# A fused decoder layer on one core: another order of instructions in the prologue, in odd self-attention turns, at the transition, in the cross maxima, at the seam and at the end

## The reference

```python
x = x + self_attention(layernorm(x), Wq, bq, Wk, bk, Wv, bv, Wo)      # 16 heads of 16; scores[0,-1] = scores[-1,0] = -1e9
q, k, v = heads(layernorm(x) @ Wq + bq), heads(ctx @ Wk + bk), heads(ctx @ Wv + bv)
energy = where(mask == 0, -1e10, q k^T / 4)
x = x + merge(softmax(energy, axis=1) @ v) @ Wo + bo                   # axis 1: over the heads
gate, up = nvfp4_linear(layernorm(x), gate_w), nvfp4_linear(layernorm(x), up_w)     # 256 -> 1024
x = x + nvfp4_linear(silu(gate) * up, down_w)                          # 1024 -> 256
```

## Time and profile before

| what | value |
|---|---|
| median of 3 runs | 567.04 us (565.94 to 567.5) |
| profiled execution, its own time | 565.97 us |
| its span | 564.2 us |
| instructions | 14,568 |
| PE, DVE, ACT, POOL busy (share of the span) | 93%, 89%, 59%, 60% |

### The profile page before, as it was taken

One profiled execution on the slowest core, in us unless ns is written; L12 is line 12 of the kernel. 1 busy time (PEld: TensorE's weight loads), 2 busy tenths in 40 slices (PEclk: granted clock), 3 DMA queues, 4 the chain that ended last, 5 costly groups with the idle time before them and its releaser, 6 DMA issues. The chain is left out here.

```text
span 564.2 us, 14568 instructions
## 1 busy us (share of the span) xinstructions
PE 523.3 (93%) x6022; PEld 374.5 (66%) x6031; DVE 499.7 (89%) x678; ACT 335.6 (59%) x559; POOL 336.4 (60%) x258
## 2 busy tenths in 40 slices
PE   7899999999899999999999999999999877878876
PEld 7777767777567777777776777777777543444433
DVE  5788888899889888889899999899889999989997
ACT  3755655655555665468475765676568464856644
POOL 3121324323327776767888879977898894745660
PEclk9999999999999999999999999999999998989998
DMA  8910000000110011101110111011100000000001
GB/s 216 319 68 2 3 1 3 3 2 1 42 40 1 12 40 48 46 4 50 49 30 21 49 48 34 18 48 48 35 17 9 9 2 17 0 21 19 20 19 57
DMA packets 16644, 20.77 MB, mean 37 GB/s; under 512 B 2821, under 2 KB 14322, under 8 KB 16578
## 3 DMA queue, kind: packets, MB, share of 16 engines
q1 hardware_dynamic: 14800, 19.18, 11.4%
q10 hardware_dynamic: 1778, 0.66, 0.6%
HBM read 16.16 MB, written 1.84 MB: 32 GB/s over the span
## 5 line engine op out<-in xcount | busy, mean ns | idle before, releaser
L435 POOL TENSOR_TENSOR work<-work,rden 125x1792 f32<-125x1792 f32 x48 | 172.5, 3593 | 3.8
L1045 ACT ACTIVATE work<-scores 125x896 f32<-125x896 f32 x96 | 88.9, 987 | 89.1 <-PE scores L1548 89.1
L715 DVE TENSOR_REDUCE negmax<-scores 125x112 bf16<-125x1792 f32 x48 | 97.1, 2023 | 17.9 <-PE scores L1538 17.2
L723 DVE TENSOR_REDUCE den<-work 125x56 f32<-125x896 f32 x96 | 102.5, 1067 | 7.7 <-ACT work L1045 7.5
L433 POOL TENSOR_TENSOR rden<-rden,stays 125x112 f32<-125x112 f32 x48 | 21.9, 457 | 62.9 <-DVE rden L728 62.8
L1538 PE MATMUL scores<-qz,kT 32*125 32x224 f32 x768 | 49.8, 373 | 3.6 <-ACT work L1045 2.9
L1574 PE MATMUL head_out<-work,v 125*32 125x112 f32 x1536 | 48.7, 265 | 0.3 <-POOL work L435 0.3
L1645 PE MATMUL wide<-ctxT,ck 128*128 128x375 f32 x128 | 48.6, 500 | 0.0
L1548 PE MATMUL scores<-negmax,identb 125*125 125x448 bf16 x192 | 45.4, 359 | 2.5 <-DVE negmax L715 2.2
L1659 PE MATMUL wide<-cv,ctxT 128*125 128x256 f32 x192 | 46.7, 379 | 0.0
L728 DVE RECIPROCAL rden<-den 125x112 f32<-125x112 f32 x48 | 40.9, 852 | 1.4
(11 more groups left out here) (283 smaller groups left out, 1132.3 us busy)
## 6 DMA issues: line engine op xcount, KB each, us to landing
ctx_sb<-in_ctx SPq DMA_DIRECT2D x16, 375.0 KB
mask_sb<-in_mask_Bx1xSxS_if SPq DMA_DIRECT2D x16, 164.1 KB, 5.5
xsx<-in_x SPq DMA_DIRECT2D x4, 448.0 KB, 10.0
out_x<-ores SPq DMA_DIRECT2D x6, 256.0 KB, 2.4
a_raw_w<-in_L_ffn_gate_w SPq DMA_DIRECT2D x1, 1024.0 KB, 8.7
a_raw_w<-in_L_ffn_up_w SPq DMA_DIRECT2D x1, 1024.0 KB, 11.2
a_raw_w<-in_L_ffn_down_w SPq DMA_DIRECT2D x1, 1024.0 KB, 13.3
xt<-xsx SPq DMA_DIRECT2D x4, 112.0 KB, 2.2
```

Of the source, the lines that this page charges most:

```text
L435: pool.tensor_tensor(ex2[0:KP, kc], ex2[0:KP, kc], over, ALU.mult).then_inc(s["prob"], 1)
L715: dve.tensor_reduce(negmax[0:KP, :], scores[0:KP, :, 0:4 * TOK].rearrange("p j (h t) -> p t j h", h=4), AX.XY, ALU.max, negate=True).then_ ...
L723: link(dve.tensor_reduce(den[0:KP, kc, half], ex2[0:KP, kc, :, half, :].rearrange("p g t s -> p t g s"), AX.XY, ALU.add))
L1045: act.activation(ex2[0:KP, kc, 4 * i:4 * i + 4].rearrange("p (j m) t s -> p j m s t", m=NE), scores[0:KP, 2 * i:2 * i + 2, 0:4 * TOK].rear ...
```

## The change

Nothing is computed in another way. Six places get another order.

- **Prologue.** The statistics, rstd and shift of batch 0 are made alone, ahead of the other three of its group (`first_statistics`, `first_shift`, semaphores `stats0`, `rstd0`, `shift0`: four more DVE instructions and one more on POOL). ACT normalises batch 0 before it copies any weight, and copies the weights of keys and values after `a_input_copy(0)`; PE waits for the first weight alone before the queries. The 16 idle products between the weight transposes and the first `a_input_T` are gone. `bias_products` and the copy of `bv_row` come one batch earlier. The values of batch 1 are copied by DVE, between `statistics(2)` and `statistics(3)`, and no longer by ACT.
- **Odd self turns** (5 to 15). The value product is cut in its two halves: the first stands before `maxima_T`, the second where both stood.
- **Transition.** ACT's `maxima_copy(15)` stands before `keys(0, 0)`, and PE's `key(0, 1, ·)` before `a_project(14)`.
- **Cross maxima.** DVE's `key_max(now, 0)` always stands before `head_sum(old, 2, 0)`. Before, it stood behind it in the turns in which no weight or tile work had been put in, which are n = 1, 2, 3, 4, 6 and 13.
- **Seam.** In turn 0 PE's `score(0, 1)` stands before `a_project(15)`, and `less_max(0, 1)` before the query and the first key of batch 1. In turn 15 DVE's `residual(14)` stands behind `inverse(15, 2)`, and both halves of `project(14)` before `less_max(15, 2)`.
- **End.** `output(4)` stands behind `rounded_last`, the end of the DVE's last rounding, and not in k = 7. The down product of pair 5 goes into a bank of its own (`y_before`), so that it doesn't wait for `output(4)`.

```diff
+def of_group(g):
+    return range(max(g * XG, 1), (g + 1) * XG)
 ...
+pool.wait_ge(a_s["stats0"], 1)
+pool.tensor_tensor(rstd[:, 0:1, 0], varp[:, 0:1], minus_half[:, 0:1], ALU.pow).then_inc(a_s["rstd0"], 1)
 for g in range(4):
     pool.wait_ge(a_s["stats"], g + 1)
-    part = slice(g * XG, (g + 1) * XG)
+    part = slice(of_group(g)[0], (g + 1) * XG)
 ...
+first_statistics()
 statistics(0)
+first_shift()
 shift(0)
 ...
 if t == 1:
     statistics(2)
+    dve.wait_ge(a_s["v_ps"], 2)
+    dve.tensor_copy(a_v[:, 1, :, 0:3:2, :], two_heads(value_ps(1))).then_inc(a_s["v"], 1)
     statistics(3)
 ...
-if old and not late:
-    head_sum(old, 2, 0)
 if now:
     key_max(now, 0)
-if old and late:
+if old:
     head_sum(old, 2, 0)
 ...
 inverse(final, 2)
+residual(in_turn(B - 2))
 hidden(0, 1)
 ...
-if k >= 3:
+if 3 <= k < NPT:
     output(k - 3)
 ...
 rounded_last()
+output(NPT - 3)
 output(NPT - 2)
 output_last(0)
 output_last(1)
 ...
+a_normal(0)
 weight_copy(0, wqT)
-weight_copy(1, wkT)
-a_normal(0)
-weight_copy(2, wvT)
 a_input_copy(0)
+weight_copy(1, wkT)
+weight_copy(2, wvT)
 ...
+maxima_copy(b)
+if t == B + 1:
     keys(in_turn(0), 0)
-maxima_copy(b)
 ...
-idle_products(16, ho_ps[:, 0:P], identb[:])
 ...
-if a == 0 and p < NPT - 1:
+if a == 0 and p < NPT - 2:
     wait(pe, s["out"], p)
+y = y_last[a] if p == NPT - 1 else (y_before if p == NPT - 2 else y_ps)[:, a, :]
 ...
 a_input_T(1)
+bias_products()
 first_projections(1)
+pe.wait_ge(a_s["bv_row"], 1)
 maxima_T(0)
 a_value(1)
 score_columns(0)
 a_input_T(2)
-pe.wait_ge(a_s["mT"], 1)
-bias_products()
 ...
+if other:
+    a_value(t, [0])
 maxima_T(b)
 ...
 if other:
-    a_value(t)
+    a_value(t, [1])
+if t == B + 1:
+    key(in_turn(0), 1, 0)
+    key(in_turn(0), 1, 1)
 a_project(b - 1)
-if t == B + 1:
-    key(in_turn(0), 1, 0)
-    key(in_turn(0), 1, 1)
 ...
+if n in (0, B - 1):
+    score(now, 1)
 if n == 0:
     a_project(B - 1)
-if n == B - 1:
-    score(now, 1)
 ...
 if new:
     input_T(new)
     context_T(new)
+if n == 0:
+    less_max(now, 1)
 if new:
     query(new)
     key(new, 0, 0)
-if now:
+if n > 0 and now:
     less_max(now, 1)
```

More of the change, by code:

```diff
@@ L180, in decoder_layer @@
         a_s = {n: sem("a_" + n) for n in (
-            "made", "aux", "rows", "link_d", "link_p", "stats", "rstd", "shift", "w_ps", "w_sb", "bv_cols", "bv_ps",
+            "made", "aux", "rows", "link_d", "link_p", "stats0", "rstd0", "shift0", "stats", "rstd", "shift", "w_ps", "w_sb", "bv_cols", "bv_ps",
             "bv_row", "xn", "biased", "xnT_ps", "xnT", "qk_ps", "pair_q_ps", "pair_q", "pair_k_ps", "qz", "v_ps", "v", "s1_ps", "max", "mT_ps", "mT", "s2_ps",
@@ L251, in decoder_layer @@
         y_ps = small[:].rearrange("p (a d) -> p a d", a=2)
+        y_before = scores[:, 0].rearrange("p (a d) -> p a d", a=2)
         y_last = (scores[:, 2, 0:D], head_out[:, 0:D])
@@ L901, in output @@
                     wait(dve, stored[p % 2], 16 * (p // 2))
-                    dve.scalar_tensor_tensor(out=ores[:, p % 2], in0=y_ps, scalar=alpha[:, 2:3],
+                    dve.scalar_tensor_tensor(out=ores[:, p % 2], in0=y_before if p == NPT - 2 else y_ps, scalar=alpha[:, 2:3],
                                              in1=xt[:, 2 * p:2 * p + 2, :], op0=ALU.mult, op1=ALU.add
@@ L1031, in a_normal @@
                 def a_normal(b):
-                    act.wait_ge(a_s["shift"], b // XG + 1)
+                    if b == 0:
+                        act.wait_ge(a_s["shift0"], 1)
+                    else:
+                        act.wait_ge(a_s["shift"], b // XG + 1)
                     wait(act, a_s["xnT_ps"], b - 1)
@@ L1252, in _ @@
                 a_normal(2)
+                act.wait_ge(a_s["bv_ps"], 1)
+                act.copy(bv_row[:], a_y_ps).then_inc(a_s["bv_row"], 1)
                 maxima_copy(0)
                 a_queries_keys(1)
-                a_values(1)
                 a_input_copy(2)
@@ L1259, in _ @@
                 a_values(2)
-                act.wait_ge(a_s["bv_ps"], 1)
-                act.copy(bv_row[:], a_y_ps).then_inc(a_s["bv_row"], 1)
                 a_normal(3)
@@ L1507, in a_project, with a_value @@
                     last.then_inc(a_s["y_ps"], 1)
-                def a_value(b):
-                    if b >= SINGLE and b % 2 == 1:
+                def a_value(b, part=range(NE)):
+                    if b >= SINGLE and b % 2 == 1 and 0 in part:
                         pe.wait_ge(a_s["v"], b)
-                    for c in range(NE):
+                    for c in part:
                         last = pe.matmul(value_ps(b), a_xnT[:, c, b % 2, :], wvT[:, c, :], start=(c == 0), stop=(c == NE - 1))
-                    last.then_inc(a_s["v_ps"], 1)
+                    if NE - 1 in part:
+                        last.then_inc(a_s["v_ps"], 1)
                 acts, projects, wide_uses, pieces_read = Count(), Count(), Count(), Count()
@@ L1773, in down @@
                             small_free()
+                    y = y_last[a] if p == NPT - 1 else (y_before if p == NPT - 2 else y_ps)[:, a, :]
                     for c in range(FF // P):
-                        last = pe.matmul(y_last[a] if p == NPT - 1 else y_ps[:, a, :], hT[:, a, c, :], downT[:, c, :],
+                        last = pe.matmul(y, hT[:, a, c, :], downT[:, c, :],
                                          start=(c == 0), stop=(c == FF // P - 1))
@@ L1781, in first_projections @@
                     if t == 0:
+                        pe.wait_ge(a_s["w_sb"], 1)
+                    projected(t, 0, wqT)
+                    if t == 0:
                         pe.wait_ge(a_s["w_sb"], 2)
-                    projected(t, 0, wqT)
                     projected(t, 1, wkT)
@@ L1888, in _ @@
                         context_T(new)
+                    if n == 0:
+                        less_max(now, 1)
+                    if new:
                         query(new)
@@ L1914, in _ @@
                         project(old, 0)
+                    if n == B - 1:
+                        project(old, 1)
                     if now:
@@ L1926, in _ @@
                     if old:
-                        for c in range(0 if n < 6 else 1, NE):
+                        for c in range(0 if n < 6 else NE if n == B - 1 else 1, NE):
                             project(old, c)
```

28 lines of the change are left out of this document (16 added, 12 removed).

## The result

The changed kernel takes 569.46 us (median of 11 runs, 568.15 to 572.3), the one before 565.98 (11 runs, 565.47 to 567.5). The ratio is 1.0055, 95% interval 1.0042 to 1.0069: slower, by more than a measurement leaves open. The two profiled executions have spans of 567.6 and 564.2, so the profile holds the whole difference (+3.4).

The account below looks back on a forecast made before the run. TensorE was taken to bound cross attention and the self turns, VectorE the feed forward and the prologue's second part. The terms -0.1, 0, -1.5, +1.1, +0.4, -0.3, +0.7 gave +0.3 on 567.04, so 567.3 us, range 565.0 to 569.7.

Parts of the forecast that it names:

- the likeliest case: Whole kernel: all terms summed with no clock fall, +0.3 us to a median of 567.3; chance 0.42.
- a clock under 1 at one of the two big waits: TensorE's 1.9 us waits for maxima, prologue and seam: a clock under 1 at either would prove the prediction wrong.
- prologue: First maxima 0.8 earlier, VectorE's value copy 0.4 more and a wait of 0.3: -0.1 us (-0.4 to +0.2).
- odd self turns: Half the value product moves ahead of the maxima on TensorE, both halves' sum unchanged: 0 us.
- transition: Earlier copies of maxima and second keys on ACT bring the first cross scores forward: -1.5 us.
- seam: Cross turn 0: the exponent's 1.35 wait goes, waits of 0.5 (residual) and 1.9 (maxima) come: +1.1 us.
- cross maxima: Later `head_sum` delays POOL's normalisation and TensorE's product with it, in turns 13 and 6: +0.4 us (0 to +0.7).
- turn 15: `residual(14)` leaves VectorE's chain into the first tiles for a place under an inverse: -0.3 us (0 to -0.43).
- end: `output(4)` leaves the rounding, but the last output steps wait 2.4 us for its store: +0.7 in place of -0.6.
- The +0.3 that the prediction set beside its own +0.7: End: alternative size of the term from the skill page's fixed cost of about 2.0 us for another kind of queue.
- DVE passes the gain on: Prologue: VectorE, hardly idle from 16.55 until the second maxima, carries the first maxima's 0.8 us gain forward.
- a rival, at 1.0 to 1.7 for one fall: New idle in prologue or at seam lowers TensorE's clock: one fall adds 1.0 to 1.7, giving 568.7; chance 0.25.

Follow-up runs that it names:

- e11: The kernel before with the transition's part of the change alone: 564.98 us, ratio 0.9969.
- e6: Changed kernel with GpSimd's additions held, 28 idle products in TensorE's remaining prologue wait, and the seam's new order in cross turn 0 taken back: 565.22 us, ratio 0.9975.
- e7: Changed kernel with GpSimd's additions held, 28 idle products, and only the seam's swap of scores and projection taken back, early `less_max` kept: 564.84 us, ratio 0.9965.
- e3: Changed kernel with 44 idle TensorE products in the long prologue wait before the transposes of the second maxima: 567.68 us, ratio 1.0025.
- e4: Changed kernel with GpSimd's additions of the value bias held back until the second row maxima are done: 566.32 us, ratio 0.9999.

## Why the prediction was right and where it was wrong

The forecast was 567.3 with a range to 569.7 and 0.3 for slower; measured was 569.46 from a kernel before that had come out 1.1 us lower than in the first three runs. The time is in the range, but the likeliest case was the wrong one: the change is 3.5 slower, not 0.3. That it is in the range is luck of the level: 3.5 on top of the 567.04 that the forecast was built on is 570.5, past its end at 569.7. By the sign that the prediction named itself, a clock under 1 at one of the two big waits, its likeliest case failed in the prologue; both waits are there, and at the seam the clock stayed at 1.00. By its terms:

| term | predicted | measured |
|---|---|---|
| prologue | -0.1 | +3.1 |
| odd self turns | 0 | +1.1 |
| transition | -1.5 | -1.8 |
| seam | +1.1 | +1.15 |
| cross maxima | +0.4 | -0.4 |
| turn 15 | -0.3 | -0.3 |
| end | +0.7 | +1.0 |
| a clock fall at 499 us that this execution didn't have | not in the sum | -0.4 |

- **Transition and seam** went as worked out, with the named waits (0.67 and 1.69 for the predicted 0.5 and 1.9). Runs e11, e6 and e7 bear out the mechanisms, and e7 the one of the seam: VectorE's written order, read together with the order on TensorE.
- **End.** The step was right, and so was its size: alone the part costs 0.67 in the trace. The store's wait is 1.62 where 1.8 was expected. The +0.3 that the prediction set beside its own +0.7 was too low: 2.3 us passed between the store's data being there and the step. In the changed kernel TensorE's last products ran at the lower clock (1.91 us for `head_out`, 1.04 in the kernel before), so the last half waited 0.24 for them. It started 0.73 behind the first half, where it is 0.40 in the run with the end alone (561.61 against 561.21), and this 0.33 is the 0.3 on top.
- **Prologue.** The term was -0.1 and +3.1 was measured. Its own parts came out better than forecast: the first maxima gained 1.14 where -0.8 was taken, the copy of the values took 0.34 from start to start, and the wait put at 0.3 wasn't there, so that with the additions held the second maxima are 0.65 early. Then two steps failed. "DVE passes the gain on" took the durations of the kernel before for those instructions and didn't ask what GpSimd would do beside them. The moved `bias_products` brought GpSimd's additions forward by 5 us onto VectorE's small copies, and 1.3 us went there. The prediction had looked at what each moved step waits for, and not at who waits for the moved step. The second is the clock. It was a rival, at 1.0 to 1.7 for one fall and 0.25 likely. It came, after an idle of 3.00 and not 1.9, and filled all of 30 to 36 us. It cost 2.4 (e3), more than the bound, because the price had been read from a stretch that was at the lower level for only part of its 7 us. Together -0.65, 1.3 and 2.4 make the 3.1.
- **How long an idle must be.** Against a fall the prediction cited the Trainium skill, "TensorE: Matmul & The Clock Gate", section "HAM oscillation — how this bites in real kernels", whose worked case has the clock fall in waits for transfers of about 3 to 5 us. The idle of 3.00 us is at the lower edge of these, and the clock fell. It also fell after 1.67 us (e4), which is well under them. So the case doesn't mark a length below which an idle is safe.
- **Odd turns.** "The sum of both halves is the same" is true of TensorE's list and beside the point, and the 0 that came of it was +1.1. The step that failed is the cover: the half that moved had hidden a wait for the exponent behind the second scores.
- **Cross maxima.** The +0.4 for POOL's late normalisation isn't there. In each of the six turns the maxima start 1.11 us behind the start of their scores where it was 1.17 (192.48 against scores at 191.31 before, 195.87 against 194.76 after), and six times this difference is the 0.4 won. Why VectorE takes them up 0.06 sooner isn't shown by any row; it was idle before them in both.

## What to carry to other kernels

A step that is moved forward also moves what waits for it, on engines that the diff doesn't name: list these followers, and look at what they will then run beside. Work that fills a wait is only free where it stands; before moving it, ask which wait it covers now, and not only which it will cover. A longer wait on TensorE can have two prices, its own and that of the clock behind it. Here the second was the larger (2.4 of 3.1 us), and a run with idle products in the gap tells them apart. And one profile shows one execution: in these profiles the clock fell at different places, so a difference of half a microsecond between medians is first held against the granted clocks of the executions.

## What the runs showed of the hardware

- **The clock doesn't follow from the length of one idle.** TensorE fell to 1.2 GHz after 3.00, 2.99 and 1.67 us of idle in the prologue. The lower level didn't begin at the same point of the wait: within it, at 29 to 30 us (0.71), in the changed kernel, and in the held run only when TensorE had been busy again for over a microsecond (0.97 busy of 29 to 30 us at 1.00, then 0.87 and 0.50). The clock didn't fall after 1.69 at the seam, with 0.67 shortly ahead of it. And it can fall without any long wait: in the profile of the transition alone it did so near 17 us, in a prologue that is the one before the change, with the same waits. Eight products, first there and then in the kernel before:

```profile
17.28 1.96 PE L1498 MATMUL wide<-a_xnT,a_wqT 128*128 128x112 f32 x8 [0.43 <-ACT a_xnT L1183]
17.27 1.15 PE L1497 MATMUL wide<-a_xnT,a_wqT 128*128 128x112 f32 x8 [0.43 <-ACT a_xnT L1183]
```

Ahead of them TensorE had been idle for 0.91 and 0.43 us in both, and `a_oT` of batch 0 was 1.52 late behind the fall.

In the feed forward the same wait of 1.98 us for `qv` was followed by a fall in some executions and by none in others. The kernel before (eight down products 1.76 us):

```profile
549.53 0.62 PE L1746 MATMUL wide<-identb,qv 128*128 128x128 bf16 x8 [1.98 <-POOL qv L492]
550.83 1.76 PE L1775 MATMUL small<-downT,hT 128*128 128x256 bf16 x8 [0.68 <-DVE ores L902]
```

and the one with the prologue alone (1.03 us):

```profile
553.13 0.62 PE L1769 MATMUL wide<-identb,qv 128*128 128x128 bf16 x8 [1.98 <-POOL qv L498]
554.43 1.03 PE L1798 MATMUL small<-downT,hT 128*128 128x256 bf16 x8 [0.68 <-DVE ores L922]
```

- **GpSimd slows VectorE's small instructions.** Beside an addition of 112 x 256 in SBUF on GpSimd, a copy of one row went from 0.21 to 0.63 us, a cast of 125 x 256 from 0.29 to 0.70, a subtraction from 0.42 to 0.75. Not every instruction beside them was hit: a cast between two of the long ones, at 24.39, took 0.28, and a copy at 26.16 took 0.22. GpSimd's additions were longer as well: 0.73 us each (three in 2.20) and 0.79 (two in 1.58) beside these instructions, against 0.66 (five in 3.29) in the kernel before. With the additions held back, all of VectorE's were short again and its maxima 1.3 us earlier, so it is the additions; by what the two engines hinder each other isn't shown.
